# Layer 0's tile pipeline of a two-layer decoder: small VectorE steps between the halves of the top-k rounds, the experts two steps behind the top-k, the projection two ahead

## The reference

```
x = x + attention(layernorm(x))                    # 16 heads of 16; output projection Wo
q = (layernorm(x) @ Wq.T + bq), 16 heads           # cross-attention on 77 context rows
scores = q . k / 4                                 # per row and head: 77 scores
top 32 of the 77 scores -> softmax over these -> times V
x = x + context @ Wo.T + bo
logits = layernorm(x) @ router_w.T + router_b      # 8 experts, top 1
x = x + (expert_w[top1] @ layernorm(x) + expert_b[top1]) * max softmax(logits)
```

## Time and profile before

| | us |
|---|---|
| runs | 1985.93, 1985.16, 1983.98; median 1985.16 |
| profiled execution | 1987.05 |
| its span | 1985.3 |
| VectorE busy | 1255.1 (63%) |
| TensorE busy | 1579.4 (80%) |
| ScalarE, GpSimd busy | 934.1 (47%), 482.1 (24%) |
| granted TensorE clock, mean | 0.878 of 2.4 GHz |

### The profile page before, as it was taken

How to read it: one execution, slowest core, us unless ns; L and a number is a source line. 1 busy time by engine, 2 the same in 40 slices (tenths; PEclk the granted TensorE clock), 3 DMA queues, 4 the chain that set the end, 5 groups by cost and what they waited for, 6 DMA issues and landing times. The chain is left out here.

```text
span 1985.3 us, 27618 instructions
## 1 busy us (share of the span) xinstructions
PE 1579.4 (80%) x8891; PEld 871.2 (44%) x8892; DVE 1255.1 (63%) x4695; ACT 934.1 (47%) x1831; POOL 482.1 (24%) x386
## 2 busy tenths in 40 slices
PE   4758999999976488889867676999987882389993
PEld 2431222222224366767656432333326761156662
DVE  6988888887407999999980356777735558401112
ACT  2731777777655445555543340666673651111110
POOL 3760000000003354455542151111111342300003
PEclk9965999999897778888878785999998995689997
DMA  6175133331010000000000059336300121741003
GB/s 196 59 203 79 21 45 44 44 45 20 25 43 1 1 1 2 1 1 1 1 1 1 6 163 170 43 44 86 44 1 1 15 41 32 254 162 33 26 24 93
DMA packets 113013, 102.91 MB, mean 52 GB/s; under 512 B 45095, under 2 KB 88171, under 8 KB 112878
## 3 DMA queue, kind: packets, MB, share of 16 engines
q1 hardware_dynamic: 111345, 97.06, 22.6%
q0 software_dynamic: 1536, 4.20, 0.7%
HBM read 67.61 MB, written 33.35 MB: 51 GB/s over the span
## 5 line engine op out<-in xcount | busy, mean ns | idle before, releaser
L1052 DVE TENSOR_REDUCE arena<-banks 128x2 f32<-128x1024 f32 (+1 forms) x448 | 481.2, 1108 | 149.7 <-PE banks L899 94.3
L988 ACT ACTIVATE arena<-banks 128x512 f32<-128x512 f32 (+3 forms) x896 | 439.9, 557 | 187.3 <-PE banks L938 180.6
L899 PE MATMUL banks<-arena 96*128 96x512 bf16 (+3 forms) x896 | 285.9, 396 | 50.1 <-DVE arena L1052 21.2
L938 PE MATMUL banks<-arena 98*128 98x512 bf16 (+3 forms) x896 | 272.0, 364 | 9.0 <-ACT arena L988 6.8
L950 PE MATMUL banks<-arena 128*32 128x512 f32 (+3 forms) x1792 | 220.8, 565 | 12.6 <-ACT arena L988 6.5
L1654 DVE MATCH_REPLACE8 arena<-arena 128x77 f32<-128x77 f32 x1024 | 213.9, 226 | 0.0
L899 PEld LDWEIGHTS banks<-arena 96*128 96x128 bf16 x896 | 80.6, 102 | 233.7 <-DVE arena L1052 136.9
L938 PEld LDWEIGHTS banks<-arena 98*128 98x128 bf16 x896 | 82.4, 98 | 188.0 <-ACT arena L988 124.1
L2433 DVE COPY arena<-banks 128x1024 f32<-128x1024 f32 x23 | 28.2, 1225 | 206.9 <-PE banks L2372 206.9
L1549 POOL TENSOR_SCALAR arena<-arena 128x256 f32<-128x256 f32 x32 | 39.1, 1223 | 476.2 <-DVE arena L1635 476.1
L1650 DVE MAX8 arena<-arena 128x8 f32<-128x77 f32 x1024 | 149.5, 225 | 1.4
(11 more groups left out here) (276 smaller groups left out, 2535.2 us busy)
## 6 DMA issues: line engine op xcount, KB each, us to landing
arena<-parts SPq DMA_DIRECT2D x192, 128.0 KB, 7.3
arena<-in_L_ffn_W SPq DMA_DIRECT2D x16, 1024.0 KB, 12.2
parts<-arena SPq DMA_DIRECT2D x24, 512.0 KB, 9.1
v<-arena SPq DMA_DIRECT2D x32, 256.0 KB, 2.3
arena<-v SPq DMA_DIRECT2D x16, 512.0 KB, 11.1
arena<-sorted SPq DMA_DIRECT2D x23, 128.0 KB, 2.1
expert_out<-arena SPq DMA_DIRECT2D x23, 128.0 KB, 1.7
sorted<-arena SPq DMA_DIRECT2D x5, 512.0 KB, 7.4
```

Source lines behind the costliest of these rows:

```text
L899: mm = pe.matmul(bank[:, 0:w], qst[r][0:KS, j, i * P:(i + 1) * P], kst[r][0:KS, j, kb * BANK:kb * BANK + w], start=True, stop=not diag)
L938: pe.matmul(bank, kst[r][0:KM, j, kt * P:(kt + 1) * P], qst[r][0:KM, j, half * BANK + lo:(half + 1) * BANK], start=True, stop=True).then_i ...
L988: act.activation(prob[:, gi % 2 * G + j, lo:BANK], PS[:, 4 + n % 3, 0:BANK - lo], ACT.Exp, scale=SCALE).then_inc(sem(s + "_exp"), 1)
L1052: dve.tensor_reduce(m2[u % 2][:, 2 * pair:2 * pair + 2, i, kb], PS[:, 2 * (n % 2):2 * (n % 2) + 2, 0:w], AX.X, ALU.max).then_inc(sem(s + " ...
```

## The change

- The loop runs from FIRST = -2 to LAST = T + 2 in place of -3 and T + 4: 20 steps in place of 23. The projection stands two tiles ahead, context, mixing, second layernorm and logits all in step t+1, router and experts in step t+2.
- In VectorE's list `largest` is cut in two, `largest` (maxima) and `taken` (replacements). The order of a step is now: maxima 0, replacements 0, router, choose, chosen, maxima 1, replacements 1, maxima 2, sums, normalize, replacements 2, gates, maxima 3, row statistics, aggregate, replacements 3, inverse.
- The lists of TensorE, ScalarE and GpSimd follow. TensorE's four `turn_weights`, `context` and `turn_context` of a tile stand together, then the spread, mixing, output and the experts, and last h1, h2 and the logits. GpSimd has h2 ahead of h1. ScalarE has `deviations` (Sqrt) behind the mixing and both exponentials ahead of it.
- The experts' result is in bank EB = 1, the logits in bank OB. The expert matrices are turned three, three and two in the first three steps.
- `ta` is computed by a tensor_tensor with a broadcast operand in place of a tensor_scalar.

The diff, cut to its core. Removed lines of the order lists are those of the listing above.

```diff
 GROUPS = ((0, 6, 0, 0), (6, 2, 1, 0), (8, 4, 1, 2 * C), (12, 4, 2, 0))
 OUTS = ((0, 0, 2, 6 * C), (12 * C, 2, 1, 4 * C))
-PB, WB, QB, OB = 3, 4, 6, 7
-FIRST, LAST = -3, T + 4
+EB, PB, WB, QB, OB = 1, 3, 4, 6, 7
+FIRST, LAST = -2, T + 2
+TURNS = (3, 3, 2)
 def inside(t):
     return 0 <= t < T
 def normed(t):
-    return [w for w, n in ((0, t + 2), (1, t - 3)) if inside(n)]
+    return [w for w, n in ((0, t + 2), (1, t - 1)) if inside(n)]
 def norms(t):
 def steps(t):
     return sum(1 for n in range(FIRST, t + 1) if normed(n))
+
+def turned(t):
+
+    n = t - FIRST
+    return range(sum(TURNS[:n]), sum(TURNS[:n + 1]))
 @block.sync
...
 def _(sp):
     def turn_attended(t):
         if t >= 1:
             pe.wait_ge(sem(s + "_x1"), t)
-        if t >= 5:
-            pe.wait_ge(sem(s + "_ot"), t - 4)
-        if t >= 6:
-            pe.wait_ge(sem(s + "_x2"), t - 5)
+        if t >= 4:
+            pe.wait_ge(sem(s + "_x2"), t - 3)
         for k in range(KD):
             mm = pe.transpose(PS[:, PB, k * P:(k + 1) * P], blocks[:, t // TB, k, t % TB, :], ident)
...
         for g in range(NG):
     def turn_context(t):
         pe.wait_ge(sem(s + "_ot"), t + 1)
-        if t >= 3:
-            pe.wait_ge(sem(s + "_yt"), t - 2)
-        elif t:
+        if t:
             pe.wait_ge(sem(s + "_n"), t)
+            pe.wait_ge(sem(s + "_lg"), t)
         for g in range(NG):
             mm = pe.transpose(PS[:, OB, g * P:(g + 1) * P], ot[t % 2][:, g, :], ident)
         mm.then_inc(sem(s + "_otp"), 1)
...
         for n in range(4 * c, 4 * c + 4):
     def experts(t, part):
         if part == 0:
-            pe.wait_ge(sem(s + "_n"), min(t + 3, T))
+            pe.wait_ge(sem(s + "_sc"), 2 * min(t + 4, T))
             pe.wait_ge(sem(s + "_ohT"), t + 1)
-            pe.matmul(PS[:, OB, 0:D], ohT, bias, start=True, stop=False)
+            pe.matmul(PS[:, EB, 0:D], ohT, bias, start=True, stop=False)
         pe.wait_ge(sem(s + "_hmT"), t * 4 + 2 * part + 2)
         for n in range(E * part, E * part + E):
-            mm = pe.matmul(PS[:, OB, 0:D], hmT[:, n, :], WeT[:, n // KD, n % KD, :], start=False, stop=(n == 2 * E - 1))
+            mm = pe.matmul(PS[:, EB, 0:D], hmT[:, n, :], WeT[:, n // KD, n % KD, :], start=False, stop=(n == 2 * E - 1))
         mm.then_inc(sem(s + "_ey"), 1)
...
     pe.wait_ge(sem("w_in"), W_IN)
     for t in range(FIRST, LAST):
         if inside(t + 1):
             query(t + 1)
...
+        if inside(t + 2):
+            turn_attended(t + 2)
         if inside(t + 1):
             scores(t + 1)
...
+        if inside(t + 2):
+            project(t + 2)
+        for e in turned(t):
+            turn_expert(e)
+        if inside(t - 1):
+            for c in range(4):
+                turn_weights(t - 1, c)
+            context(t - 1)
+            turn_context(t - 1)
         if inside(t - 2):
...
+            turn_choice(t - 2)
+            for c in range(4):
+                turn_spread(t - 2, c)
+        if inside(t - 1):
+            turn_mixed(t - 1)
+            output(t - 1)
         if inside(t - 2):
...
+            experts(t - 2, 0)
+            experts(t - 2, 1)
         if inside(t + 2):
             turn_h1(t + 2)
...
         if inside(t - 1):
...
+            turn_h2(t - 1)
+            logits(t - 1)
 @block.scalar
...
         act.wait_ge(sem(s + "_d"), t + 1)
             queries(t + 1)
         if inside(t - 1):
             exp_left(t - 1)
...
+        if inside(t + 2):
+            attended(t + 2)
+        if inside(t + 1):
+            copy_scores(t + 1)
+        if inside(t + 2):
+            attended_rows(t + 2)
+        for e in turned(t):
+            act.wait_ge(sem(s + "_wep"), e + 1)
+            act.copy(WeT[:, e].rearrange("p k n -> p (k n)"), PS[:, WB + e % 2, :]).then_inc(sem(s + "_weT"), 1)
+        if inside(t - 1):
+            for c in range(4):
+                copy_weights(t - 1, c)
+            context(t - 1)
+        if inside(t - 2):
+            router_exp(t - 2)
+        if inside(t):
+            exp_all(t)
+        if inside(t - 2):
+            choice(t - 2)
+            for c in range(4):
+                copy_spread(t - 2, c)
+        if inside(t - 1):
+            mixed(t - 1)
+            mixed_rows(t - 1)
         if normed(t):
             deviations(t)
...
         if inside(t - 2):
...
+            gated(t - 2)
         if inside(t + 2):
             turned_h1(t + 2)
...
         if inside(t - 1):
...
+            turned_h2(t - 1)
 @block.gpsimd
...
 def _(pool):
         return pool.tensor_tensor(dst, src, m8[t % 2][:, 0, :, 0:1].to_broadcast([P, NH, C]), ALU.subtract)
     def normal(dst, t, w):
...
+        return pool.tensor_scalar(dst, x[:, t + 2 - 3 * w, :], mv2[t % 2][:, w, 0:1], sd[t % 2][:, w:w + 1],
                                   ALU.subtract, ALU.mult)
     for t in range(FIRST, LAST):
         if inside(t - 1):
             pool.wait_ge(sem(s + "_topped"), t * NH)
             less_max(left[(t - 1) % 2], left[(t - 1) % 2], t - 1).then_inc(sem(s + "_d2"), 1)
...
             pool.wait_ge(sem(s + "_e2"), t)
             pool.wait_ge(sem(s + "_e"), t)
             n = (t - 1) % 2
             pool.tensor_tensor(ex[n], ex[n], left[n], ALU.subtract).then_inc(sem(s + "_w"), 1)
+        if inside(t):
+            pool.wait_ge(sem(s + "_m"), (t + 1) * NH)
+            if t >= 2:
+                pool.wait_ge(sem(s + "_wtp"), (t - 1) * 4)
+            less_max(ex[t % 2], sc[t % 2], t).then_inc(sem(s + "_d"), 1)
+        if inside(t - 2):
+            pool.wait_ge(sem(s + "_oh"), t - 1)
+            if t == 2:
+                pool.wait_ge(sem(s + "_wep"), E)
+            else:
+                pool.wait_ge(sem(s + "_hmp"), 4 * (t - 2))
+            n = (t - 2) % 2
+            pool.tensor_tensor(hm, h2[n].unsqueeze(1).to_broadcast([P, E, D]),
+                               oh[n].unsqueeze(2).to_broadcast([P, E, D]), ALU.mult).then_inc(sem(s + "_hm"), 1)
         if normed(t):
             pool.wait_ge(sem(s + "_rstd"), steps(t))
+        if inside(t - 1):
+            if t >= 3:
+                pool.wait_ge(sem(s + "_hp2"), t - 2)
+            normal(h2[(t - 1) % 2], t, 1).then_inc(sem(s + "_h2"), 1)
         if inside(t + 2):
             if t >= 0:
                 pool.wait_ge(sem(s + "_hp1"), t + 1)
             normal(h1[t % 2], t, 0).then_inc(sem(s + "_h1"), 1)
             pool.tensor_tensor(x[:, t + 2, :], x[:, t + 2, :], xb_out, ALU.add).then_inc(sem(s + "_xb"), 1)
...
+        if inside(t - 2):
+            pool.wait_ge(sem(s + "_yt"), t - 1)
+            pool.tensor_tensor(x[:, t - 2, :], x[:, t - 2, :], yt[(t - 2) % 2], ALU.add).then_inc(sem("e0_x"), 1)
 @block.vector
...
 def _(dve):
         n = t % 2
         dve.wait_ge(sem(s + "_lp"), t + 1)
-        dve.tensor_tensor(lg[n], PS[:, QB, D:D + E], br[0], ALU.add).then_inc(sem(s + "_lg"), 1)
+        dve.tensor_tensor(lg[n], PS[:, OB, 0:E], br[0], ALU.add).then_inc(sem(s + "_lg"), 1)
         dve.wait_ge(sem(s + "_lg"), t + 1)
         dve.tensor_reduce(m1[n], lg[n], AX.X, ALU.max).then_inc(sem(s + "_lmax"), 1)
     def choose(t):
         n = t % 2
         dve.wait_ge(sem(s + "_lmax"), t + 1)
-        dve.tensor_scalar(ta[n], lg[n], m1[n], None, ALU.subtract).then_inc(sem(s + "_ta"), 1)
+        dve.tensor_tensor(ta[n], lg[n], m1[n].to_broadcast([P, E]), ALU.subtract).then_inc(sem(s + "_ta"), 1)
         dve.scalar_tensor_tensor(out=eo[n], in0=lg[n], scalar=m1[n], in1=order, op0=ALU.is_equal,
                                  op1=ALU.mult).then_inc(sem(s + "_eo"), 1)
...
         dve.wait_ge(sem(s + "_eo"), t + 1)
     def row_statistics(t):
         for w in normed(t):
...
+            n = t + 2 - 3 * w
             dve.wait_ge(sem(s + ("_x1", "_x2")[w]), n + 1)
             dve.bn_stats(st[t % 2][:, w, :], x[:, n, :]).then_inc(sem(s + "_st"), 1)
         src = (sc if k == 0 else left)[r]
         for hd in range(NH):
             dve.max(m8[r][:, k, hd, :], src[:, hd, :]).then_inc(sem(s + "_m" if k == 0 else f"{s}_m{k}"), 1)
+
+    def taken(t, k):
+        r, hn = t % 2, t * NH
+        src = (sc if k == 0 else left)[r]
         dve.wait_ge(sem(s + "_m" if k == 0 else f"{s}_m{k}"), hn + NH)
         dve.memset(cell[:, r, 2 * k + 1:2 * k + 2], 0.0)
         for hd in range(NH):
                           rs[t % 2].unsqueeze(2).to_broadcast([P, NH, HD]), ALU.mult).then_inc(sem(s + "_n"), 1)
     for t in range(FIRST, LAST):
...
+        if inside(t):
+            largest(t, 0)
+            taken(t, 0)
+        if inside(t - 2):
+            router(t - 2)
+            choose(t - 2)
+            chosen(t - 2)
+        if inside(t):
+            largest(t, 1)
+            taken(t, 1)
+        if inside(t):
+            largest(t, 2)
+        if inside(t - 1):
+            sums(t - 1)
+            normalize(t - 1)
+        if inside(t):
+            taken(t, 2)
+        if inside(t - 2):
+            gates(t - 2)
+        if inside(t):
+            largest(t, 3)
```

(63 more changed lines are left out.)

95 lines of the change are left out of this document (16 added, 79 removed).

## The result

The changed kernel takes 1992.39 us (median of 17 runs), before 1985.49 us (17 runs): ratio 1.0036, interval 1.0025 to 1.0046. That is +6.9 us; +9.5 was forecast.

The account below looks back on a forecast made before the run. VectorE, nearly full in layer 0's tile pipeline, was taken as the bound, TensorE close behind. Fill, steps and drain gave 743.4 + 13 P; P = 29.4 makes +9.5 us on 1985.16: 1994.7 us, range 1970 to 2010.

Parts of the forecast that it names:

- The wait at `sums` and its chain: Dependent work from `inverse` to `sums`: ready at 17.7 us, wanted at 15.1, so VectorE waits 2.65 us a step.
- the five points of the chain: h1 and h2 done at 2.5 us, queries' copy 6.7, table load 8.0, subtraction 12.1, `sums` ready 17.7.
- VectorE's own side: VectorE's own work in a changed step: 15.1 us up to `sums` and 11.15 behind it, 26.3 us.
- s: Time in us within a step, counted from the end of `inverse`, where the next maxima start.
- The mean step: Steps 2 to 14: 5 of 13 at 30.3 us, the others at 28.9, mean 29.4 us.
- the 1.2 GHz level: TensorE at half clock from projection to output: statistics 1 us late, 0.4 for weights and context, step 30.3 us.
- the second bound: TensorE in half-clock steps: experts end at 33 us, just as the next step's h1 is there.
- Small steps between the halves: VectorE's small operations fill three of four gaps between halves; its own work was put 0.5 us above before's.
- Port lock: VectorE's `ta` blocked by GpSimd's `less_max`: the new form is no remedy, but costs nothing under the wait at `sums`.
- My rival: `less_max` slips behind `ta`, uncovered: 13 x 2.27 = 30 us, 1982 us; chance inside the 0.18 for in-between chains.
- Fill: Stretch before the first maxima: VectorE starts at 611 us against 608, 3 us lost.
- drain: Stretch after the last round: 54 us in place of 85.9, a gain of 32 us called sure.

Follow-up runs that it names:

- e1: The changed kernel with one small unused Exp on ScalarE right behind each step's Sqrt, making the table load run earlier: ratio to before 0.995, 1973.25 us.
- e6: The changed kernel with GpSimd making h1 ahead of h2, nothing else: ratio to before 0.9983, 1980.49 us.
- e7: The kernel before, at its old depth, with VectorE's small steps between the halves and inverse behind the maxima of round 2: ratio 1.0001, 1984.24 us.
- e8: The changed kernel with h1 first, less_max ahead of the residual additions, query ahead of h2's turn, and e1's Exp: ratio to before 1.0146, 2013.58 us.
- e9: e8 with the router's sums and numbered choice kept in TensorE's bank OB in place of SBUF: ratio to before 0.9906, 1964.3 us.
- e11: e7 with the small Exp right behind ScalarE's Sqrt, so the table load runs early: ratio to before 0.9932, 1971.05 us.
- e3: The changed kernel with six matmuls a step whose result nobody reads, in TensorE's gaps: ratio to before 1.0086, 2000.48 us.

## Why the prediction was right

- *The wait at `sums` and its chain.* Right to 0.1 us at each of the five points of the chain read above. VectorE's own side was 0.4 us too long: it came to `sums` at s = 14.9, not 15.1, and needed 10.9 us behind it, not 11.15. So its work in a step is 25.8 us, as before the change, not 26.3. 28.75 us for a step at full clock (28.9 forecast); e1 and e6 shortened the chain in two places and the step followed.
- *The mean step.* 29.48 us over steps 2 to 14, 29.4 forecast, but for a partly wrong reason, so that the closeness is in part luck. I placed the 1.2 GHz level at spread, mixing and output. In the trace most long steps have it at the query and the scores. The short step above has it in the spread (3.54 us), yet its rows are copied by 1004.91, only 0.1 us after the statistics before them began. So there it cost that step nothing. But the experts ended 1 us later for it, and the turn of the next h1 was 0.3 us late: the second bound that the forecast named, at a smaller price. Each of the three steps with a late turn has such a spread in the step before. At the head of the chain the 1.2 GHz level cost up to 1.3 us. Size right, place mostly wrong.
- *Small steps between the halves.* Forecast as no gain of their own; e7 shows it for the old depth. The new depth with the old order of the small steps was not run, so their part in the changed kernel is open.
- *Port lock.* Right that the new form of `ta` is no remedy. In the changed kernel's last steps (VectorE, GpSimd):

```profile
1070.02 1.60 DVE L1584 TENSOR_TENSOR arena<-arena 128x8 f32<-128x8 f32 x1
```

```profile
1069.33 2.26 POOL L1528 TENSOR_TENSOR arena<-arena 128x1232 f32<-128x1232 f32 x1
```

The Trainium skill's rule (SBUF — State Buffer, "Who interferes with whom"), that an operation with two SBUF inputs waits for a GpSimd operation that reads SBUF, is borne out by this row and by e8 against e9: the trace agrees. Right also that it costs nothing here: `less_max` ended as `ta` began in most steps, and up to 0.4 us in three others went under the wait at `sums`. My rival priced it at one block, 2.27 us; e8 had two in a row, 4.4.
- *Fill and drain.* Fill +1.4 for +3, drain 51.1 for 54, where I had added 1 us for half clock and had spread, mixing and output at 6.8 us where they took 5.6. Their errors add to 4.5 us and the rounds' is 0.6 the other way: these are the terms that put the forecast too high, by 3.9 us against this trace and by 2.6 against the medians. No term is off by more than 3 us.
- *Where the 34.8 us of the drain went.* Into the rounds. A shorter pipeline asks more of one step: with e1's Exp in both, the new depth (0.995) is no better than the old one with interleaving (e11, 0.9932).

## What to carry to other kernels

When a software pipeline is made shallower, write down when each moved result is wanted and when its chain can deliver it; a drain saved once buys only so much per step: here 34.8 us of drain, over 16 steps, is 2.2 us a step, and the steps lost 2.4. Look along that chain for things that are not work: a table load behind an unrelated copy, an engine's queue order. Before moving an operation into another engine's time, look at which operands it has in SBUF.

## What the runs showed of the hardware

- A VectorE operation with both inputs in SBUF stood until GpSimd's operation had ended: 0.17 us became 2.51, and 0.22 became 2.30 (e8); the same operations with their first input in the accumulators took 0.17 and 0.22 inside GpSimd's subtraction (e9, at 1021.35). GpSimd's operations were no longer for it (2.79 and 2.78 us). The profile shows it as a long operation, not as a wait.
- A little less waiting went with a steady clock on TensorE. A step of the changed kernel and one of e1 differ by 1.4 us of waiting; the one shows the 1.2 GHz level at the query in seven of thirteen steps, the other nowhere from 727 to 1027 us. It is not a rule: e9's steps are as short as e1's (27.3 us) and have the 1.2 GHz level at the spread in each, and e3, with matmuls in the waits, has it at the turn of the context.
